# Cross-attention with 20 heads: PV writes head pairs into even and odd rows of each 32 row block, and 4 DMAs bring them to natural order instead of 12

## The reference

```python
q = heads(x @ Wq); k = heads(ctx @ Wk); v = heads(ctx @ Wv)
p = softmax(q @ k.T / sqrt(16))            # over the 77 keys, per head
x = merge(p @ v) @ Wo + bo + x             # then the same again with the second layer's weights
```

## Time and profile before

| | us |
|---|---|
| runs (3), median | 929.22 |
| runs, fastest and slowest | 926.53, 930.88 |
| profiled execution, first to last instruction (span) | 926.1 |
| TensorE busy in it | 903.4 |
| VectorE, ScalarE, GpSimd busy | 685.7, 544.6, 402.8 |

### The profile page before, as it was taken

The page is one execution under the profiler, slowest core; times in us unless marked ns, Lnnn a source line. Parts: engine busy times, 40 slices in busy tenths (PEclk is TensorE's granted clock), DMA queues, the critical chain, the costliest instruction groups (busy, mean ns, idle before and its releaser), DMA issues.

```text
span 926.1 us, 28090 instructions
## 1 busy us (share of the span) xinstructions
PE 903.4 (98%) x11518; PEld 681.3 (74%) x11518; DVE 685.7 (74%) x1221; ACT 544.6 (59%) x549; POOL 402.8 (43%) x229
## 2 busy tenths in 40 slices
PE   8899999999999999999999999999999999999897
PEld 5777778777787777777777777777778777777665
DVE  3775787868778686787868688786786868678557
ACT  4456565656556556666556656556665656656553
POOL 3424263633436263366624446364344625433224
PEclk9999999999999999999999999999999999999999
DMA  6313534445444544545555444544534544443342
GB/s 203 102 32 80 138 93 132 135 124 148 98 119 119 164 131 110 149 115 140 141 148 140 102 118 113 137 132 123 134 95 118 139 131 134 102 130 78 86 134 94
DMA packets 80526, 112.41 MB, mean 121 GB/s; under 512 B 21200, under 2 KB 37878, under 8 KB 80400
## 3 DMA queue, kind: packets, MB, share of 16 engines
q1 hardware_dynamic: 80208, 110.35, 44.4%
q10 hardware_dynamic: 192, 0.26, 0.2%
HBM read 60.24 MB, written 22.24 MB: 89 GB/s over the span
## 4 chain that ended last, share of the span: by engine, by line
PE 82%; DVE 6%; DMA 4%; SPq 3%; issue 2%; ACT 1%; POOL 1%; DVEq 0%; ACTq 0%; POOLq 0%
PE pR L307 27%; PE pR L444 14%; PE pA L391 10%; PE pR L378 8%; PE pR L287 4%; PE pR L329 4%; PE pR L257 4%; DMA X<-in_xT 2%; PE pA L397 2%; PE pR L261 2%; DVE OS L1090 2%; SPq L1434 1%; PE pA L307 1%; DVE QL L995 1%; PE pR L244 1%
## 5 line engine op out<-in xcount | busy, mean ns | idle before, releaser
L763 ACT ACTIVATE P<-pA 77x2048 f32<-77x2048 f32 x160 | 300.4, 1878 | 197.2 <-PE pA L397 196.9
L1034 DVE TENSOR_REDUCE Mx<-pR 128x4 f32<-128x308 f32 (+1 forms) x480 | 259.2, 575 | 31.8 <-PE pR L378 26.6
L1293 POOL TENSOR_TENSOR On<-On,OS 128x1024 f32<-128x1024 f32 (+1 forms) x58 | 105.8, 1845 | 257.8 <-DMA OS<-rd 257.8
L307 PE MATMUL pR<-OS,Wo 128*128 128x512 f32 x638 | 168.1, 402 | 2.9 <-DVE OS L1090 2.1
L444 PE MATMUL pR<-P,VA 77*17 77x256 f32 x2480 | 157.4, 385 | 0.8 <-ACT P L763 0.5
L378 PEld LDWEIGHTS pR<-KH,QH 32*128 32x128 f32 x1280 | 96.3, 183 | 70.8 <-issue 46.6
L391 PE MATMUL pA<-QH,KH 32*77 32x256 f32 x1280 | 145.0, 291 | 0.1
L1258 POOL TENSOR_TENSOR XS<-X,XS 128x1024 fp32r<-128x1024 f32 x31 | 74.0, 2387 | 152.1 <-ACT XS L649 152.1
L378 PE MATMUL pR<-KH,QH 32*128 32x154 f32 x1280 | 131.5, 283 | 7.8 <-DVE X L1101 2.2
L307 PEld LDWEIGHTS pR<-OS,Wo 128*128 128x128 f32 x638 | 113.8, 188 | 33.2 <-issue 6.3
L391 PE MATMUL pA<-QL,KH 32*77 32x256 f32 x1280 | 134.9, 275 | 0.0
(11 more groups left out here) (161 smaller groups left out, 1289.6 us busy)
## 6 DMA issues: line engine op xcount, KB each, us to landing
On<-Oraw SPq DMA_DIRECT2D x244, 64.0 KB, 2.7
OS<-rd SPq DMA_DIRECT2D x58, 256.0 KB
C<-in_cT SPq DMA_DIRECT2D x16, 616.0 KB, 7.9
X<-in_xT SPq DMA_DIRECT2D x16, 512.0 KB
y<-X SPq DMA_DIRECT2D x16, 512.0 KB, 4.0
X<-y SPq DMA_DIRECT2D x16, 512.0 KB
out<-X SPq DMA_DIRECT2D x15, 512.0 KB, 4.0
X<-in_xT SPq DMA_DIRECT2D x16, 256.0 KB
```

The lines of the kernel that those rows point to most:

```text
L307: f = pe.matmul(p[:, :], W[:, k, c0:c0 + 128], S[:, s, :], start=(i == 0), stop=(i == len(pairs) - 1))
L763: act.activation(P[0:L, i % PR, :, :], pA[0:L, :, :], ACT.Exp, scale=float(D) ** -0.5).then_inc(p_done, 1)
L1034: dve.tensor_reduce(Mx[:, :, :].rearrange("p t (j i) -> p j t i", j=4)[:, j:j + banks, :, i:i + 2], pR[:, bank:bank + banks, 0:2 * LK].rea ...
L1293: pool.tensor_tensor(On[rows, blocks, :], On[rows, blocks, :], recips(u, part).bitcast(F32), ALU.mult).then_inc(o_mul, 1)
```

## The change

PV takes 32 columns of VA for each head instead of 17. VA now has ten ones ahead of the values and ten behind them, and the heads stand in another order within a channel (even heads in places 10 to 17, odd ones in 0 to 7, heads 16 to 19 in 18, 19, 8, 9). With a step of 10 the even heads' values fall on rows 0, 2, .. 30 of the block of 32 and their sum on row 31, the odd heads' on rows 1, 3, .. 31 with the sum on row 0; the rows between hold products that nothing reads. On keeps the interleaved order of each pair of heads, and the rows of Wo are put in the same order on the host. In Oraw the groups stand in the order 0, 2, 1, 3, 4.

The DMAs of a unit then are: natural 1 + 1 + 2, sums 1 + 1 + 2, spread 4 + 1 (one for each m and parity, to 64 partitions each, with 4 heads by 16 copies). `sums(r)` takes the groups 0 and 2 or 1 and 3. In even units `sums(u, 0)` moves from the end of unit u to the begin of unit u + 1, behind `sums(v, 2)`. `V_last` issues six activations instead of two.

```diff
-                        f = pe.matmul(bank[32 * j:32 * j + D + 1, b * SQ:b * SQ + SQ], VA[0:L, u % 2, b, h:C + H:H], src,
+                        f = pe.matmul(bank[32 * j:32 * j + 32, b * SQ:b * SQ + SQ], values_and_one(u, b, h), src,
...
+            def columns(t, first, step):
+                return bass.AP(t.tensor, t.offset + first, [list(t.ap[0]), [step, 32]])
+            def values_and_one(u, b, h):
+                g = HPOS[h]
+                return columns(VA[0:L, u % 2, b, :], HH + g if g >= HH else g, HH)
...
+                for h in range(16, H):
+                    g = HPOS[h]
+                    act.activation(halves[:, h % 2, :, g:g + 1], v[:, :, g:g + 1], ACT.Copy)
                 for p in range(2):
-                    f = act.activation(VN[0:KT[t], t - 1, p * C:p * C + C].rearrange("p (d h) -> p d h", h=H)[:, :, p:H:2],
-                                       VS[0:KT[t], t, :].rearrange("p (d h) -> p d h", h=H)[:, :, p:H:2], ACT.Copy)
+                    heads = slice(HPOS[p], HPOS[p] + 8)
+                    f = act.activation(striped[:, :, p, heads], v[:, :, heads], ACT.Copy)
...
             def odd_heads(u):
...
-                for j in range(4):
-                    act.dma_start(On[32 * j + D:32 * j + 2 * D, 0:2, :],
-                                  Oraw[32 * j:32 * j + D, 1:4:2, :]).then_inc(d_on[1], 16)
+                act.dma_start(On[ODD, 0:2, :], Oraw[ODD, 2:4, :]).then_inc(d_on[1], 16)
...
             def recip_last(u):
-                dve.wait_ge(d_zt, 16 * (u + 1))
+                dve.wait_ge(d_zt, 32 * (u + 1))
...
-            def sums(u, m):
+            def sums(u, r):
-                z = Oraw[D:128:32, :, :].rearrange("p q c -> p (q c)")
-                for k in range(2 * m, min(2 * m + 2, NG)):
+                for k in ((0, 2), (1, 3), (4,))[r]:
                     sp.wait_ge(o_raw[k][u % 2], u // 2 + 1)
-                if m < 2:
+                if r < 2:
...
-                    sp.dma_start(Zg[64 * m:64 * m + 64, :],
-                                 z[:, 2 * m * N:(2 * m + 2) * N].rearrange("p (i c) -> p i c", c=64)).then_inc(d_zg, 16)
+                    z = Oraw[31 * (1 - r):128:32, 2 * r:2 * r + 2, :].rearrange("p q c -> p (q c)")
+                    sp.dma_start(Zg[64 * r:64 * r + 64, :], z.rearrange("p (i c) -> p i c", c=64)).then_inc(d_zg, 16)
                 else:
...
-                    sp.dma_start(Zt[:, :], z[:, 4 * N:5 * N].rearrange("p (i c) -> p i c", c=64)).then_inc(d_zt, 16)
+                    for i, row in enumerate((31, 64)):
+                        sp.dma_start(Zt[16 * i:16 * i + 16, :],
+                                     Oraw[row:row + 33:32, 4, :].rearrange("p (i c) -> p i c", c=64)).then_inc(d_zt, 16)
...
-                    for j in range(4):
-                        sp.dma_start(On[32 * j + D * r:32 * j + D * r + D, 0:2, :],
-                                     Oraw[32 * j:32 * j + D, r:r + 3:2, :]).then_inc(d_on[r], 16)
+                    sp.dma_start(On[(EVEN, ODD)[r], 0:2, :], Oraw[(EVEN, ODD)[r], 2 * r:2 * r + 2, :]).then_inc(d_on[r], 16)
...
-                for j in range(4):
-                    sp.dma_start(On[D * j:D * j + D, 2, :], Oraw[32 * j:32 * j + D, 4, :]).then_inc(d_ont, 16)
+                sp.dma_start(On[0:32, 2, :], Oraw[0:64:2, 4, :]).then_inc(d_ont, 16)
+                sp.dma_start(On[32:64, 2, :], Oraw[65:128:2, 4, :]).then_inc(d_ont, 16)
...
-                for m in ((0, 1), (2,))[part]:
-                    src = a["rd"][u, 8 * m * N:min(8 * m + 8, H) * N].rearrange("(h o c) -> h o c", o=1, c=N)
-                    sp.dma_start(recips(u, part)[:, m % 2, :].bitcast(F32),
-                                 src.broadcast_to([MT[m] // D, D, N])).then_inc((d_rb, d_rbt)[part], 16)
+                if part == 0:
+                    for m in range(2):
+                        for p in range(2):
+                            src = a["rd"][u, 8 * p * N:8 * p * N + 8 * N].rearrange("(j m o c) -> m j o c", m=2, o=1, c=N)
+                            sp.dma_start(recips(u, part)[(EVEN, ODD)[p], m, :].bitcast(F32),
+                                         src[m].broadcast_to([4, D, N])).then_inc(d_rb, 16)
+                    return
+                src = a["rd"][u, 16 * N:H * N].rearrange("(h o c) -> h o c", o=1, c=N)
+                sp.dma_start(recips(u, part)[:, 0, :].bitcast(F32), src.broadcast_to([4, D, N])).then_inc(d_rbt, 16)
...
                     load_c(u // 2 + 2)
-                    sums(u, 0)
                     load_x(u + 3)
                 else:
                     sums(v, 2)
+                    sums(v, 0)
                     sums(v, 1)
```

More of the change, by code:

```diff
@@ L30 @@
 QC = 2 * N + SQ
+OSLOT = (0, 2, 1, 3, 4)
+HH = H // 2
+HPOS = [HH * (1 - h % 2) + h // 2 for h in range(16)] + [18, 19, 8, 9]
 WORDER = ["Wk0", "Wq0", "Wv0", "Wo0", "Wk1", "Wv1", "Wq1", "Wo1"]
@@ L81, in build @@
         VS = sb("VS", [128, 3, C])
[L82 removed]
+        VA = sb("VA", [128, 2, 2, HH + C + HH])
         Vt = sb("Vt", [KT[2], C])
@@ L96, in build @@
         mask = sb("mask", [128, 2])
-        small = sb("small", [128, 4 * D])
-        ones = small[0:L, :].rearrange("p (a d) -> p a d", a=2)
-        Zt = small[96:128, :]
+        small = sb("small", [128, 34 + 3 * D])
+        stripes, blocks = small[0:L, 0:34], small[0:L, 34:34 + 3 * D]
+        Zt = small[96:128, 0:4 * D]
         bias = sb("bias", [128, 2, 3])
@@ L174, in last_o @@
             return OL[:, m, :] if m < 2 else OL2[:, :]
+        EVEN, ODD = slice(0, 128, 2), slice(1, 128, 2)
         count = {}
@@ L471, in PV_last @@
                                 first = half == 0
-                            f = pe.matmul(dst, VL[0:L, b, h:2 * C:H] if what == "OL" else ones[:, pp, :], src,
+                            g, vl = HPOS[h], VL[0:L, b, :]
+                            if what == "ZL":
+                                lhs = stripes[:, pp:pp + 32] if m < 2 else blocks[:, D * pp:D * pp + 32]
+                            else:
+                                lhs = columns(vl, g, H)
+                            f = pe.matmul(dst, lhs, src,
                                           start=first, stop=True, skip_group_check=True)
@@ L770, in o_copy @@
                 if u and k < 4:
-                    act.wait_ge(d_on[k % 2], 64 * u)
+                    act.wait_ge(d_on[k % 2], 16 * u)
                     act.wait_ge(d_zg, 32 * u)
                 elif u:
-                    act.wait_ge(d_ont, 64 * u)
-                    act.wait_ge(d_zt, 16 * u)
-                act.activation(Oraw[:, k, :], psum(slot["PV", u, k])[:, :], ACT.Copy).then_inc(o_raw[k][u % 2], 1)
+                    act.wait_ge(d_ont, 32 * u)
+                    act.wait_ge(d_zt, 32 * u)
+                act.activation(Oraw[:, OSLOT[k], :], psum(slot["PV", u, k])[:, :], ACT.Copy).then_inc(o_raw[k][u % 2], 1)
             def split_o(u, part):
@@ L1043, in o_copy @@
                 if u and k < 4:
-                    dve.wait_ge(d_on[k % 2], 64 * u)
+                    dve.wait_ge(d_on[k % 2], 16 * u)
                     dve.wait_ge(d_zg, 32 * u)
                 elif u:
-                    dve.wait_ge(d_ont, 64 * u)
-                    dve.wait_ge(d_zt, 16 * u)
-                dve.tensor_copy(Oraw[:, k, :], psum(slot["PV", u, k])[:, :]).then_inc(o_raw[k][u % 2], 1)
+                    dve.wait_ge(d_ont, 32 * u)
+                    dve.wait_ge(d_zt, 32 * u)
+                dve.tensor_copy(Oraw[:, OSLOT[k], :], psum(slot["PV", u, k])[:, :]).then_inc(o_raw[k][u % 2], 1)
             def recip(u):
@@ L1286, in normalise @@
                     for r in range(2):
-                        pool.wait_ge(d_on[r], 64 * (u + 1))
-                    pool.wait_ge(d_rb, 32 * (u + 1))
+                        pool.wait_ge(d_on[r], 16 * (u + 1))
+                    pool.wait_ge(d_rb, 64 * (u + 1))
                 else:
-                    pool.wait_ge(d_ont, 64 * (u + 1))
+                    pool.wait_ge(d_ont, 32 * (u + 1))
                     pool.wait_ge(d_rbt, 16 * (u + 1))
@@ L1300, in split_o @@
                 pool.tensor_tensor(OS[:, 3:5, :], On[:, 0:2, :], OS[:, 0:2, :].bitcast(F32), ALU.subtract).then_inc(o_lo, 1)
-            pool.memset(VA[:, :, :, C:C + H].rearrange("p a b c -> p (a b) c"), 1.0)
+            for c in (0, HH + C):
+                pool.memset(VA[:, :, :, c:c + HH].rearrange("p a b c -> p (a b) c"), 1.0)
             pool.memset(CS[:, :, L4:L4 + 12].bitcast(F32), 0.0)
             for p in range(2):
-                pool.memset(ones[:, p, D * p:D * p + D], 1.0)
-                pool.memset(ones[:, p, D - D * p:2 * D - D * p], 0.0)
+                pool.memset(stripes[:, p:34:2], 1.0 - p)
+            for i in range(3):
+                pool.memset(blocks[:, D * i:D * i + D], 1.0 - i % 2)
             pool.memset(Mx[:, :, :], 0.0).then_inc(pads, 1)
@@ L1400, in values @@
                         if u < NU - 1:
```

(8 more changed lines are left out.)

6 lines of the change are left out of this document (4 added, 2 removed).

## The result

The changed kernel takes 1007.01 us, the median of 4 runs (1005.64 to 1013.26). The kernel before, beside it on the same chip, took 930.05 us (926.53 to 932.15). The ratio is 1.083 with a 95% interval of 1.078 to 1.088. The forecast was 973 with a range of 933 to 996: the sign was right, and the loss of 77 us is 1.8 times the forecast one, and the time lies 11 us above the range.

The account below looks back on a forecast made before the run. TensorE, busy 98% of the span, was taken as the bound, so only its idle time could be won. 926.5 + 3.2 + 34 + 5.7 + 1.4 = 970.8, plus 2.7 to the median, told as 973; range 933 to 996.

Parts of the forecast that it names:

- The spread's lateness: Spread of the reciprocals: four engines instead of eight carry twice as much each, taking 2.8 us longer.
- the 9.5 that I gave as a sign: Sign of being right: the store's 128 KB land some 9.5 us after issue, where it was 6.7.
- the forecast 0.25: Sign of being right: a DMA share of 0.25 right after the spread's first issue; 0.50 would be wrong.
- In even units 2.8 us are hidden under TensorE's other projections.: Normalised output in even units: its 2.8 us of lateness cost nothing, being covered by other TensorE work.
- The stall at L384 behind out: TensorE waits for out, behind recip_last and the late sums: 2.4 us in fourteen odd units, 34 us.
- the clock falls as well: Rival, chance 0.13: stalls in dense work halve TensorE's clock, fourteen stretches adding 21 us, 994 in all.
- the 4.6 of PV and V_last: TensorE's PV weight loads, 3.2 us, and V_last's added activations, 1.4 us, together.
- The forecast 3.2 us: PV on TensorE: 108 weight loads after a wait, each 0.03 us longer with 32 strided columns.
- The late projections: Projections waiting for output of units spread in odd ones: 1.9 us later, paid three times, 5.7 us.
- SP's queue: SP's DMA issues: 5 fewer, about 3.3 us of SP per unit, worth little.
- V_last's 1.4 us: V_last: four more activations ahead of exponentials TensorE waits for, 0.34 us each, 1.4 us.

Follow-up runs that it names:

- e6: Changed kernel with four copies of each reciprocal row in DRAM, so two spreads have 16 rows outermost (16 engines): 933.76 us, 1.002 of the kernel before.
- e2: Kernel before, with each spread DMA of eight heads cut into two of four heads: 997.20 us, 1.072 of the kernel before.
- e7: Changed kernel with two spreads of 256 KB from one copy of the reciprocal rows, four engines each: 986.37 us, 1.064 of the kernel before.
- e10: e7 with the doubled channels of X loaded by two plain DMAs of 128 KB: 955.52 us, 1.026 of the kernel before.
- e4: Changed kernel with VectorE's split_o moved behind the three copies of PV's output in even units: 1018.62 us, 1.097 of the kernel before.
- e12: e6 with the doubled channels of X loaded by two plain DMAs: 930.69 us, 0.999 of the kernel before.
- e8: Changed kernel with two copies of the reciprocal rows, the spread on four engines in even units only, eight in odd: 984.88 us, 1.060 of the kernel before.
- e1: Changed kernel with eight heads outermost in the spread again, output not the reference's: 927.98 us, 0.997 of the kernel before.
- e14: Changed kernel with X's doubled channels loaded by two plain DMAs and split_o behind the copies in even units: 970.58 us, 1.039 of the kernel before.

## Why the prediction was wrong

**The spread's lateness: right.** Forecast 2.8 us from the earlier trace rows, measured 2.9 in unit 14 and in the median (6.5 to 9.4). The store's 128 KB land 8.6 us after their issue (6.7 in the earlier trace rows), short of the 9.5 that I gave as a sign, because SP issues the store 1.3 us further behind the spread's first issue (476.55 - 472.79 = 3.76, before 441.31 - 438.86 = 2.45), so that less of the delay counts as the store's own. The share of 0.24 is the forecast 0.25. By the Trainium skill, "DMA: Bandwidth & Descriptors", section "Why a DMA increments its semaphore by 16 and not by 1", four engines were to work on it; the trace agrees, with 0.24 and 87 GB/s against 0.50 and 188, and e6's sixteen rows agree in that the normalising began 2.2 us earlier than with eight.

**The step that failed first: "In even units 2.8 us are hidden under TensorE's other projections."** That looked only at TensorE's projections, which do come later. The normalised output has another reader: VectorE's split_o, ahead of the copies of PV's output in the same engine's order. The prediction never followed that path. The trace of before had the row for it: the copies ran right behind the split (451.50 + 2.35 = 453.85, next start 453.88), and TensorE's L378 came at 454.72, 0.84 us behind their start. In the kernel after, where it waited, it came 0.83 us behind it (490.12 to 490.95). The same distance of 0.84 us stands in all fourteen even units of the kernel before, with a wait of 0.31 us in just one of them. So before the change TensorE was already arriving just as its bank came free, and there was no slack behind the split at all. What arrived there was not the forecast 2.8 us of lateness either: the split waited 0.51 us for its input, and VectorE's own operations beside POOL's took most of the other 1.7. It is visible only if one looks at the distance, for a wait of zero length stands in no table.

**The stall at L384 behind out: right in mechanism, wrong in being the first.** I had 34 us in fourteen waits. e2 and e7 show it with 28.8 in 15 and 28.0 in 14, and e10 takes it away with the edit of the load. In the kernel after, the copies' wait comes before it in each pair of units and covers it (32.4 us against 4.4); with the copies' wait gone, e4 has it with 26.9 us. Since only one of them is paid, the idle time is not their sum: 34 + 5.7 = 39.7 us were forecast as idle, and TensorE's idle time grew by 48.8.

**The term that was left out of the sum: the clock.** This is the largest part of what the sum missed: it had nothing for slower work, and the page shows 29.5 us. The rival "the clock falls as well" had 0.13 and 21 us. It was the case: TensorE's busy time grew by 29.5 us on the same instructions, with 72 us at 1.2 GHz. I had argued against it that the half clocks before stood around light work; what TensorE did before the clock fell was 1.97 us of work in 4.0 there and 2.70 in 4.0 in unit 14 of the kernel after, in the middle of dense work. The clock is back where both waits are gone (1.000 in e12), but it does not go by the amount of idle time: e7 has 0.983 with 40.8 us more of it, e8, whose wait is the one for the copies, 0.967 with 30.3. The clock was never changed by itself, so 29.5 is a reading of the page and not an experiment. With that rival as the forecast the centre would have been 994. The other 13 us are 9.1 more of idle time (48.8 - 39.7) and 8.5 more of slow work (29.5 - 21), less the 4.6 of PV and V_last that do not show.

**The small terms.** The weight loads of PV (ns min/median/max of the line in the kernel after):

```profile
L461 PEld LDWEIGHTS pR<-P,VA x2480: 132/138/180, 56.2 to 964.2; 77*32 77x32 f32 x191
```

138 ns, as in the strided row. The rule of the Trainium skill, "SBUF — State Buffer", section "Specifications (TRN2)", that every crossing of a 16 byte line pays, would have a step of 40 bytes pay as one of 80, and the trace agrees. The forecast 3.2 us do not show: e1 keeps these loads and loses nothing. The late projections (three waits of L313 for the split) took 6.3 us, 2.1 before, so 4.2 of the forecast 5.7. Worth little, as said, was SP's queue: e1 has it all and gains 1.1 us, which is within what can be told. V_last's 1.4 us were not tested by themselves. Two bounds of the prediction do not follow from its own numbers: 17 us less than 973 is 956 and not 950, and at 3.4 us of lateness the stall is 14 x (3.4 - 0.4) = 42 us and not 48. Neither changes the forecast.

**What stays open.** How the 19 us between e7 and after divide between the longer split, the two more issues and the clock, and why the reciprocals come 0.8 us later in after and 0.4 earlier in e2, all three on four engines; how much of each loss is idle time that would have been there at full clock. A kernel that keeps TensorE working through the wait was not tried.

## What to carry to other kernels

Before a broadcast is cut by another index, look at what stands outermost: here 16 rows in place of 8 won nothing and 4 cost 6 to 8 per cent. When something becomes late by x, list every instruction that reads it, or what is made from it, on every engine, with what is queued behind each, and take the one with the least slack; if you find one wait, assume that others stand behind it, since in three kernels here (e4, e10, e14) removing one left or uncovered the next. And where short stalls land in the middle of dense matmul work, price the lower clock with them: here TensorE was busy 60 us longer for every 100 more of idle time (29.5 to 48.8), and from 42 (e4) to 84 (e8) in the other kernels that lost over 2 per cent.

## What had not been expected of the hardware

The same split_o of VectorE, 64x512, took 0.68 to 0.79 us in most odd units, 1.43 to 1.49 in most even ones of e7, 2.35 and 3.35 in the two timelines above, and 6.36 in one unit of the kernel after (422.47). In the even ones POOL worked beside it nearly without a gap, in e7 too, so it is not only whether POOL works but which of its operations and when they begin, and that was not taken apart. The mean over the kernel went from 1569 to 2133 ns, 17.5 us more of VectorE's time with no instruction more; what differs between the two kernels at that place is where the split lies beside POOL's work. That a delay upstream also lengthens the operation that waits for it was in no term of mine.
